# Upper f16 halves of the experts' weights, cast on ACT instead of POOL

## The reference

```python
x = x + xattn0(layernorm(x), ctx)      # 8 heads of 64, softmax over 512 context tokens
x = x + ffn0(layernorm(x))             # 128 -> 512 -> 128, piecewise-linear gelu on a 1/256 grid
x = x + xattn1(layernorm(x), ctx)      # 16 heads of 8, then relu(out @ W1 + b1) @ W2 + b2
x = x + moe(layernorm(x))

def moe(x):                            # 8 experts, top 2 of 8
    probs = softmax(t @ Wg)
    top_v, top_i = top_k(probs, 2)     # weights of the two, normalised to sum 1
    for e in range(8):
        h = silu(t @ W1[e]) * (t @ W3[e])
        out = out + comb[:, e:e+1] * (h @ W2[e])
```

## Time and profile before

| | us |
|---|---|
| Median of 3 runs (lowest, highest) | 451.77 (451.18, 452.14) |
| The profiled execution | 449.94 |
| its span, first to last instruction | 447.8 |
| PE busy | 381.1 (85%) |
| DVE busy | 323.1 (72%) |
| ACT busy | 241.6 (54%) |
| POOL busy | 195.3 (44%) |

### The profile page before, as it was taken

One profiled execution on the slowest core, in us unless ns is written; L12 is line 12 of the kernel. 1 busy time (PEld: TensorE's weight loads), 2 busy tenths in 40 slices (PEclk: granted clock), 3 DMA queues, 4 the chain that ended last, 5 costly groups with the idle time before them and its releaser, 6 DMA issues.

```text
span 447.8 us, 8284 instructions
## 1 busy us (share of the span) xinstructions
PE 381.1 (85%) x2778; PEld 220.3 (49%) x2778; DVE 323.1 (72%) x668; ACT 241.6 (54%) x473; POOL 195.3 (44%) x252
## 2 busy tenths in 40 slices
PE   8667789999779868996997899998999789999930
PEld 3414444665356445553544355553454456777620
DVE  5765594667785799779888998789851685677752
ACT  3614455655734552467476666764676444665530
POOL 5135987726464493744418134660540015015014
PEclk9957999999899989998999699998999999999985
DMA  6572708008106106422043105420030002412112
GB/s 184 129 195 53 173 1 196 16 16 197 37 1 192 58 0 151 109 72 71 25 133 91 48 5 153 113 74 2 31 108 1 6 24 62 124 37 67 40 38 64
DMA packets 44766, 34.67 MB, mean 77 GB/s; under 512 B 5965, under 2 KB 41229, under 8 KB 44429
## 3 DMA queue, kind: packets, MB, share of 16 engines
q1 hardware_dynamic: 43701, 32.03, 27.6%
q0 software_dynamic: 1024, 2.10, 1.6%
HBM read 15.11 MB, written 7.86 MB: 51 GB/s over the span
## 4 chain that ended last, share of the span: by engine, by line
PE 51%; DVE 18%; issue 9%; ACT 8%; DMA 6%; POOL 4%; SPq 4%; POOLq 0%; DVEq 0%; ACTq 0%
PE p_sc L606 7%; PE p_misc L576 5%; PE p_o L625 5%; DVE mx L879 4%; PE p_misc L507 4%; PE p_misc L781 4%; PE p_sc L781 4%; PE p_o L638 4%; SPq L1434 4%; PE p_o L792 3%; PE p_misc L800 3%; PE p_misc L533 2%; DMA slots_in<-qx,kx 2%; DVE xn L849 2%; ACT probs L1190 2%
## 5 line engine op out<-in xcount | busy, mean ns | idle before, releaser
L879 DVE TENSOR_REDUCE mx<-p_misc 128x1 f32<-128x512 f32 x192 | 122.4, 683 | 26.3 <-PE p_misc L576 25.2
L1190 ACT ACTIVATE probs<-p_sc 128x512 f32<-128x512 f32 x192 | 104.5, 597 | 57.0 <-PE p_sc L606 56.4
L576 PE MATMUL p_misc<-kS,qS 96*128 96x512 f16 x128 | 40.9, 393 | 6.4 <-DVE mx L879 6.3
L606 PE MATMUL p_sc<-qS,kS 128*128 128x256 f16 x256 | 42.1, 283 | 3.2 <-ACT probs L1190 2.6
L1304 POOL TENSOR_SCALAR veps<-meanvar 128x2 f32<-128x2 f32 x16 | 3.8, 235 | 90.9 <-DVE meanvar L835 90.5
L1346 POOL TENSOR_TENSOR psums<-probs 128x256 f32<-128x256 f32 x32 | 24.7, 773 | 42.1 <-PE p_o L632 39.2
L638 PE MATMUL p_o<-probs,v 128*32 128x256 f32 x512 | 41.3, 401 | 0.4 <-issue 0.3
L625 PE MATMUL p_o<-probs,v 128*64 128x256 f32 x256 | 35.1, 395 | 4.0 <-ACT probs L1190 3.9
L1101 DVE TENSOR_TENSOR probs<-probs,p_sc 128x512 f32<-128x512 f32 x30 | 20.6, 686 | 24.4 <-ACT probs L1268 24.1
L1372 POOL DMA_INDIRECT probs<-slots_out,kx x16 | 15.2, 948 | 50.4 <-DMA slots_out<-probs 40.1
L606 PE MATMUL p_sc<-region 128*128 128x256 f16 x256 | 35.8, 286 | 0.9 <-DVE region L893 0.9
(11 more groups left out here) (206 smaller groups left out, 741.5 us busy)
## 6 DMA issues: line engine op xcount, KB each, us to landing
region<-kx SPq DMA_DIRECT2D x24, 256.0 KB, 3.9
v<-in_L_ffn_W_dram SPq DMA_DIRECT2D x24, 256.0 KB, 2.8
region<-qx SPq DMA_DIRECT2D x24, 128.0 KB, 3.9
slots_in<-qS SPq DMA_DIRECT2D x2, 960.0 KB, 7.0
slots_out<-probs SPq DMA_DIRECT2D x30, 64.0 KB, 1.5
kS<-kS SPq DMA_DIRECT2D x1, 1664.0 KB
kS<-k_scratch SPq DMA_DIRECT2D x8, 192.0 KB
kS<-slots_in SPq DMA_DIRECT2D x6, 256.0 KB, 3.4
```

Source lines behind the costliest of these rows:

```text
L576: pe.matmul(ps, q[:, i * P:(i + 1) * P], k, start=True, stop=True).then_inc(full, 1)
L606: last = pe.matmul(p_sc[:, half, j * S:(j + 1) * S], k[:, kt * P:(kt + 1) * P], q, start=(i == 0), stop=(i == len(pairs) - 1))
L879: dve.tensor_reduce(mx[:, b % 2, i, h:h + 1], ps, AX_X, ALU.max).then_inc(free, 1)
L1190: act.activation(probs[:, h % 8, half * 512:(half + 1) * 512], p_sc[:, half, :], ACT.Exp, scale=(DH0 if layer == 0 else DH1) ** -0.5).then ...
```

## The change

The cast of each block moves from POOL's `split(c)` to a new `split(c)` of ACT, at the same place of the list. ACT now waits for the block's DMA and signals `stage_cast`; POOL waits for that and only subtracts. SP's part is unchanged: it still waits for the subtraction.

```diff
+        def halves_of(c):
+
+            w, e = (c % 2, c // 2) if c < 2 * E else (2, c - 2 * E)
+            if w < 2:
+                return ew[w][:, e, 0, :], ew[w][:, e, 1, :], stage[:, c % 2, :]
+            return ew2[:, e, :, 0, :], ew2[:, e, :, 1, :], stage[:, c % 2, :].rearrange("p (f n) -> p f n", f=FF)
...
+            def split(c):
+
+                high, low, whole = halves_of(c)
+                act.wait_ge(ld_stage[c % 2], 16 * (c // 2 + 1))
+                act.copy(high, whole).then_inc(stage_cast, 1)
...
-            steps = {"split_w": split_w, "cT": context, "k0": keys0, "v0": values0, "xT": xt, "q0": queries0, "rows": rows, "sc": softmax, "av": outputs,
+            steps = {"split": split, "split_w": split_w, "cT": context, "k0": keys0, "v0": values0, "xT": xt, "q0": queries0, "rows": rows, "sc": softmax, "av": outputs,
...
             def split(c):
 
-                w, e = (c % 2, c // 2) if c < 2 * E else (2, c - 2 * E)
-                pool.wait_ge(ld_stage[c % 2], 16 * (c // 2 + 1))
...
-                link(pool.tensor_copy(high, whole))
+                high, low, whole = halves_of(c)
+                pool.wait_ge(stage_cast, c + 1)
                 pool.tensor_tensor(low, whole, high, ALU.subtract).then_inc(stage_free, 1)
                 pool.wait_ge(stage_free, c + 1)
```

More of the change, by code:

```diff
@@ L433, in build @@
         ld_stage = sems("ld_stage", 2)
-        stage_free = sem("stage_free")
+        stage_free, stage_cast = sem("stage_free"), sem("stage_cast")
         stack_copied = sem("stack_copied")
```

## The result

The changed kernel took 469.41 us (median of 4 runs, 468.70 to 469.73), the kernel before 451.69 beside it. The ratio is 1.0383 (95% interval 1.0364 to 1.0402): slower by 17.7 us. Forecast were 15.0 us more and 466.8 us; the range of 458 to 471 holds it. In a second comparison on another occasion the same kernel had 470.03 against 454.05, 1.0324 (1.028 to 1.0368), so ratios of different occasions are compared with care, and the parts are read from the traces.

The account below looks back on a forecast made before the run. PE led (85% busy, 51% of the chain of waits) and POOL hardly set the end. Terms 4.9 + 0.6 + 0.6 + 1.0 + 5.8 + 2.9 - 0.8 = 15.0 us on 451.8 gave 466.8 us, range 458 to 471.

Parts of the forecast that it names:

- The first wait: ACT stands at cast 0 until block 0's DMA lands, delaying PE behind xT: 4.9 us (4.3 to 7.1).
- Casts 1 and 2 and the others: ACT's added casts: 0.6 us each for 1 and 2 on the path, 1.0 for those in gaps (0 to 3).
- DVE's relief: DVE steps in the FFN no longer slowed beside POOL's casts: 0.8 us back, bounds 0 to 8.
- The second wait: ACT stands at cast 16 because subtraction 13 makes SP late with block 16: 5.8 us (3.2 to 7.5).
- the clock: PE's tensor clock halves for about 3 us behind each of the two waits: 1.45 us twice, 2.9 in all.
- Rival A: Only one wait arises, as block 16 is there or SP's lateness costs nothing: 459.5 us, chance 0.12.
- Rival B: More waits: POOL's layer norms behind subtractions that wait for ACT, and casts in full: 473 us, chance 0.11.
- Rival C: Neither wait arises; 2.2 us of casts stand against DVE's relief, 450 us at five relieved steps, chance 0.04.
- The expert stage: The part of the span after the changed stretch, foreseen as equal in length before and after.

Follow-up runs that it names:

- e1: Changed kernel with casts 0 and 1 later on ACT, to take the first wait away: 464.75 us, ratio 1.0272 to the kernel before.
- e5: Kernel before, with ACT only waiting for each block where the changed kernel casts it; POOL still casts and subtracts: 461.16 us, ratio 1.0220.
- e6: Kernel before, with 24 casts of the same size added on ACT into a scratch tile, no wait for blocks: 454.14 us, ratio 1.0057.
- e3: Changed kernel with the edits of e1 and e2 together, so neither wait is left: 456.64 us, ratio 1.0076 to the kernel before.
- e9: e3 with cast 9 three exponentials later on ACT: 456.60 us, ratio 1.0048 to the kernel before.
- e4: Changed kernel with 22 unused matmuls on PE ahead of each of the two waits: 469.24 us, ratio 1.0326 to the kernel before.
- e11: Changed kernel with cast 13 two exponentials earlier on ACT: 464.23 us, ratio 1.0194 to the kernel before.
- e2: Changed kernel with casts 16 to 21 later on ACT and two POOL layer norms ahead of subtractions 19 and 20: 462.36 us, ratio 1.0185.
- e12: The changed kernel again, unedited, run beside e9 to e11: 470.03 us, ratio 1.0324 to the kernel before.
- e7: Kernel before, with POOL's cast of each block replaced by a shorter memset to zero, ACT left alone: 449.81 us, ratio 0.9963.
- e10: e9 with casts 0 to 3 also later on ACT: 453.80 us, ratio 0.9989 to the kernel before.
- e8: As e4, but at the first wait 18 unused matmuls into another PSUM bank: 472.82 us, ratio 1.0450 to the kernel before.

## Why the prediction was right

**The first wait, 4.9 us.** Measured 4.4 at the first matmul of ffn0. The block landed 2.68 us behind its issue (194.46 to 197.14) where 2.99 had been taken; ACT's work from the start of the cast to the end of `xT` took 2.84 us where 3.09 had been counted; PE's dependence on `xT` held. e1 shows its worth: 4.0 us at the Gelu of batch 3. (At the send it is 5.9, but 1.2 of that is the third loss, which differs between executions.)

**Casts 1 and 2 and the others, 0.6 + 0.6 + 1.0 us.** These were too high. The shift rises from 4.4 to 6.3 at the second bias; in e5, which has the wait and no cast, it rises from 3.7 to 5.4, so 1.7 us of this is the half clock (1.45 forecast) and cast 1 adds 0.3 at most. From the Gelu of batch 2 to that of batch 3 it changes by -0.2, and e6 finds all 24 casts to cost 0.4 us at the send. The bound of 0 for the casts in ACT's gaps was nearer than the 1.0 chosen; ACT waits for PE before most exponentials, and that PE's next scores had enough lead is how I read it, not a thing that was tested.

**DVE's relief, 0.8 us.** The size was met and the sign of the whole was not. In the first grid, batch 2, the steps that had taken 1.04, 1.53 and 1.22 us beside POOL took 0.69, 0.69 and 1.23, 1.2 us less: that is the fall from 6.3 to 5.2. In batch 3 the stretched L933 of the earlier trace rows is 1.23 now. But the contention has moved to the second half of that grid, and behind it the changed kernel loses 4.2 us in both of its traces. This is the step of the forecast that failed, though its range held: it counted which DVE steps would get away from POOL and not which ones the later subtractions would now meet, and it priced a meeting by the 0.8 us on DVE and not by PE's gap and half clock behind it. e3 against e9 shows the contention by taking it away; e4 shows that without the half clock it costs 0.7 us. So 0.8 us of the loss is the contention's in every run, and the rest is there when the clock is at half for longer behind it, which one trace can't promise for the next execution.

The Trainium skill (SBUF — State Buffer, section "SBUF: two separate sides") says that a DVE instruction with two SBUF inputs or in a 2-port mode and a GpSimd instruction take turns at a shared pair of ports, each for its whole length. The rows agree to within 0.3 us: L946, subtraction 9 and L947 follow each other from 256.24 to 259.55, 3.3 us, against 1.22 + 1.16 + 1.22 = 3.6 if nothing overlapped. The prediction drew from this rule only the gain; by the same rule a POOL instruction that is moved gains where it was and loses where it comes to lie.

**The second wait, 5.8 us, and the clock, 2 x 1.45.** Measured 6.75 us from `h1` to `h1`, clock included, against 5.8 + 1.45 = 7.25. The way there was as told: the bounce 13.8 us later than in the earlier trace rows with a shift of 9.2 just before, so 4.6 of its own (forecast: 5); block 16 was 2.5 us late of its own at its issue (forecast 2.6 to 3.6), landing 4.66 us behind it (4.9 taken). e11 shows that subtraction 13 is the cause of the lateness, and e5's 3.7 us is the loss without it (the lower bound was 3.2). The clock fell at both places, as foreseen; its price was 1.7 us at the first (e5, above), and the 1.9 us at the second rest on e4 alone. The warning of the Trainium skill that the forecast cites (TensorE: Matmul & The Clock Gate) stands there in the section "Why this matters for your kernels".

**Sum and rivals.** Forecast 15.0, measured 17.4 at the first matmul of the experts. Up to the Gelu of batch 3 it is 5.0, where the first wait, its clock, the casts and the relief had been counted at 7.7 in all; the second wait with its clock is 0.5 less than counted. Against these 3.2 us too much stand the 4.2 of moved contention and 1.4 us between the `h1` of batch 1 and the experts, which were missing. That the forecast came within 2.7 us of the 17.7 is in part because these offset each other: that is luck. Rival A (one wait) is refuted by e3 against e1 and e2. Rival B's norms behind POOL's subtractions cost at most 0.7 us between `h1` of batch 0 and the first exponential of batch 2 (the norm behind subtraction 11 starts 0.50 us behind DVE's call, where it was 0.16) and 0.8 between the `h1` of batch 1 and the send. Rival C, in which no wait arises, is out: ACT waited for both blocks.

**The expert stage** was to be equal, and in the traces it is not quite. From the first expert matmul to the end of the span it is 104.45 us before, 107.0 in the changed kernel (e12 too), 106.4 to 107.1 in the other kernels that cast on ACT without added matmuls, and 105.2 to 105.8 in e5 to e7. Between the seventh and the ninth slot ACT has longer pauses, put down to PE or to nothing that the profile names ("remote"), here in e12:

```profile
394.16 0.60 ACT L1281 ACTIVATE probs<-p_misc 128x512 f32<-128x512 f32 x1 [1.60 <-PE p_sc L788]
396.34 0.59 ACT L1287 CAST probs<-p_o 128x512 f16<-128x512 f32 x1 [1.58 <-remote]
```

Before, ACT has no such pause there. But one trace stands for the kernel before, taken 1.8 us below its median, and e10 speaks against a real cost: its stage is 106.6 us long, its send within 0.2 us of before, and yet its median is no higher than that of the kernel before; 2.1 us more would be 0.5%, outside its interval. That fits an expert stage that is short in the one trace of the kernel before and not in its usual executions; neither this nor the cause of the pauses was tested.

## What to carry to other kernels

Work that waits for a transfer is cheap on an engine that has nothing else to do there, however slow it is. Put into the list of an engine that feeds the others, it costs its wait, not its work: here 14.8 us of casts were worth 0.4 to 2.6 us (e6), and the two waits 9 us by themselves (e5). Before moving it, lay the issue and the landing of each transfer beside the time at which the new engine's list comes by; place it behind the landing, and look at what the freed engine's remaining work now lies next to. With eleven casts put a few places later, and two norms ahead of POOL's subtractions, the same change was free.

## What the runs showed of the hardware

A 128x1024 step of DVE on f32 in SBUF took up to 0.93 us longer beside a POOL subtraction, of whichever kind it was: 0.69 to 1.53 (1.62 in e10) for a one-input step, 1.22 to 2.06 for a two-input one. The subtraction is stretched as well, from 1.16 to 1.40 us in the changed kernel and to 2.07 in e4. Reductions of DVE from PSUM keep their 684 ns: those that met a subtraction in the changed kernel took 675 to 693, all of them 672 to 694.

A gap of 1.4 to 1.5 us on PE was followed by a half clock in e8 and by none in e4, on near equal work ahead of it; so, in these runs, the granted clock can't be told from the gap alone.
